# Mixing weights on four row quarters of the systolic array, in the opening of an adaLN + FFN kernel on one Trainium2 core

## What is computed

```python
# mixing by condition, the part that the change touches
h = gelu(cond_128 @ W0 + b0); h = gelu(h @ W1 + b1)
att = softmax(h @ W2 + b2)                       # 64 x 8
agg_w = einsum('bk,koi->boi', att, weight)       # 64 x 32 x 32, the mixing weights
agg_b = att @ bias_k                             # 64 x 32
y = einsum('boi,bih->boh', agg_w, x) + agg_b[:, :, None]
# gated FFN with quantised weights and low-rank parts, 512 -> 1376 -> 512
qlinear(v) = v @ ((q - 7.5) * scale * 0.005).T + 0.02 * (v @ A @ B)
x = x + qlinear_down(silu(qlinear_gate(y)) * qlinear_up(y))
# grouped convolution of 9 taps along the width, context added, then an fp8 linear layer
x = x + fp8_linear(conv(x) + ctx + bias)
```

## Time and profile before

| | us |
|---|---|
| median of three runs | 373.33 |
| the profiled execution | 373.0 |
| its span, first to last instruction | 371.2 |
| TensorE busy | 361.3 |
| VectorE busy | 243.1 |
| ScalarE busy | 190.3 |
| GpSimd busy | 78.7 |
| share of the chain that ended last, TensorE | 93% |

### The profile page before, as it was taken

One profiled execution on the slowest core, in us unless ns is written; L12 is line 12 of the kernel. 1 busy time (PEld: TensorE's weight loads), 2 busy tenths in 40 slices (PEclk: granted clock), 3 DMA queues, 4 the chain that ended last, 5 costly groups with the idle time before them and its releaser, 6 DMA issues.

```text
span 371.2 us, 5798 instructions
## 1 busy us (share of the span) xinstructions
PE 361.3 (97%) x2209; PEld 301.0 (81%) x2210; DVE 243.1 (65%) x409; ACT 190.3 (51%) x345; POOL 78.7 (21%) x68
## 2 busy tenths in 40 slices
PE   7999999999999999999999999999999999998994
PEld 3777887999888879998888789988888899997331
DVE  4949989436576664265766642737888822688995
ACT  5667797202656653035555641345667510066972
POOL 4000000021222332111422241113233221142040
PEclk9999999999999999999999999999999999999999
DMA  7997693495220000222200002326000299968288
GB/s 230 344 270 245 192 299 119 152 302 87 42 44 0 0 2 1 44 42 42 44 1 2 0 0 33 52 44 155 0 3 1 65 276 279 195 153 195 85 188 267
DMA packets 82476, 41.72 MB, mean 112 GB/s; under 512 B 52417, under 2 KB 72785, under 8 KB 82321
## 3 DMA queue, kind: packets, MB, share of 16 engines
q1 hardware_dynamic: 69072, 37.70, 37.4%
q10 hardware_dynamic: 12624, 1.82, 3.1%
q0 software_dynamic: 752, 1.84, 2.8%
HBM read 26.55 MB, written 14.80 MB: 111 GB/s over the span
## 4 chain that ended last, share of the span: by engine, by line
PE 93%; DVE 4%; ACT 1%; issue 1%; DVEq 0%
PE ps L675 44%; PE ps L660 25%; PE ps L690 6%; PE ps L608 4%; PE ps L710 3%; PE ps L870 3%; PE ps L666 2%; PE ps L712 2%; PE ps L850 1%; PE ps L623 1%; PE ps L568 1%; DVE v_plus L1506 1%; DVE q_fp L1525 1%; DVE amax L1383 0%; DVE v_plus L1513 0%
## 5 line engine op out<-in xcount | busy, mean ns | idle before, releaser
L660 PE MATMUL ps<-down_w,h_hi 128*128 128x288 f32 (+1 forms) x352 | 76.2, 297 | 0.0
L660 PE MATMUL ps<-down_w,h_lo 128*128 128x288 f32 (+1 forms) x352 | 74.7, 293 | 0.0
L675 PE MATMUL ps<-x_hi,gate_w 128*128 128x512 f32 (+1 forms) x176 | 69.9, 397 | 0.0
L675 PE MATMUL ps<-x_lo,gate_w 128*128 128x512 f32 (+1 forms) x176 | 69.6, 396 | 0.0
L675 PE MATMUL ps<-x_hi,up_w 128*128 128x512 f32 (+1 forms) x176 | 69.6, 396 | 0.0
L675 PE MATMUL ps<-x_lo,up_w 128*128 128x512 f32 (+1 forms) x176 | 69.3, 394 | 0.0
L1146 POOL TENSOR_TENSOR h_lo<-a_buf,h_hi 128x512 fp32r<-128x512 f32 (+1 forms) x33 | 42.7, 1295 | 90.0 <-ACT h_hi L984 90.0
L660 PEld LDWEIGHTS ps<-down_w,h_hi 128*128 128x128 f32 (+1 forms) x352 | 57.2, 189 | 1.1
L660 PEld LDWEIGHTS ps<-down_w,h_lo 128*128 128x128 f32 (+1 forms) x352 | 56.1, 188 | 0.0
L1435 DVE TENSOR_TENSOR a_buf<-a_buf,b_buf 128x512 f32<-128x512 f32 (+1 forms) x44 | 49.0, 1113 | 9.2 <-ACT a_buf L1050 8.1
L1157 POOL TENSOR_TENSOR x_nat<-y_buf,x_nat 128x512 f32<-128x512 f32 x15 | 20.8, 1385 | 117.0 <-DVE y_buf L1314 117.0
(11 more groups left out here) (196 smaller groups left out, 486.5 us busy)
## 6 DMA issues: line engine op xcount, KB each, us to landing
x_nat<-in_x SPq DMA_DIRECT2D x4, 1024.0 KB, 6.9
out<-x_nat SPq DMA_DIRECT2D x15, 256.0 KB, 4.5
turned<-x_nat SPq DMA_DIRECT2D x12, 256.0 KB, 3.3
x_nat<-in_down_q SPq DMA_DIRECT2D x11, 256.0 KB, 4.0
x_nat<-in_gate_q SPq DMA_DIRECT2D x10, 256.0 KB, 6.4
x_nat<-in_up_q SPq DMA_DIRECT2D x10, 256.0 KB, 6.6
edges<-zeros SPq DMA_DIRECT2D x4, 512.0 KB, 9.3
xt_own<-turned SPq DMA_DIRECT2D x6, 256.0 KB, 3.4
```

Source lines behind the costliest of these rows:

```text
L660: last = mm(ps[:, 4 + 2 * (j % 2) + m, 0:HALF + R], part[0:k, ic, j * P:(j + 1) * P], down_w[0:k, ic, m, :], start=first, stop=end)
L675: last = mm(ps[0:k, bank(ic, 2 * m), :], w[:, H * ic + c * k:H * ic + (c + 1) * k], part[:, c, :], start=c == 0 and part is x1_hi, stop=c ...
```

## The change

The mixing weights are made on four quarters of 32 rows of the array. Both factors are laid out on 128 partitions, the four stacked sums once for each quarter r; quarter r of the weights holds the output channels 4o + r, and each matrix has its 32 input channels four times side by side, once for each batch of a group. So the matmul of quarter r and block o, into bank r, gives on every band of 32 partitions the weights that this batch's block of `mix` needs, and one copy per band takes all four quarters: four copies of 32 × 128 for the first tile, two on each engine, and four of 32 × 384 for the other tiles, right behind them, straight from the banks.

With it: `cond_w_parts` is made from 128 × 256 values; the zeros in `att` go, and a column of the condition pack (`att_kept`) takes their part in a new product `att_whole`; both transposes have the same input, and ScalarE's copy waits for the first alone. GpSimd's subtraction of `lr_b` also waits for `att_bias`. The four fillers behind the bias go. The chunk of `condition(0)` that goes to bank 3 waits for the four later copies. ScalarE copies `agg_b` between its two later copies and makes the high part of `lr_a` after them. On VectorE two conversions and the low part of `lr_a` move from before the first split to behind it, the third conversion behind the second split. `mix_kept` is no longer written in the opening.

```diff
-MIX_BANK, BIAS_BANK = 5, 4
-FIRST_BANK = (6, 3, 7, MIX_BANK)
+TURN_BANKS, BIAS_BANK = (6, 5), 4
+FIRST_BANK = (6, 5, 7, 3)
...
+OC = S // OB
...
-        def mix_cells(src, q, b, g0, g1):
-            cells = src[q * S:(q + 1) * S, :].rearrange("p (o g b) -> p b g o", g=GROUPS, b=GB)[:, b, g0:g1]
-            blocks = mix[b * S:(b + 1) * S, g0:g1, b * S:(b + 1) * S].rearrange("p g (o q) -> p q g o", q=OB)[:, q]
-            return blocks, cells
+        def mix_cells(b, g0, g1):
+            cells = ps[b * S:(b + 1) * S, 0:OB, :].rearrange("p r (o g b) -> p b g o r", g=GROUPS, b=GB)[:, b, g0:g1]
+            return mix[b * S:(b + 1) * S, g0:g1, b * S:(b + 1) * S].rearrange("p g (o r) -> p g o r", r=OB), cells
...
# TensorE
-            pe.wait_ge(att_zero, 1)
-            for at, to in ((PARTS // 2, 3), (0, 2)):
-                nc.tensor.transpose(ps[0:STACKED, to, 0:B], att[:, at:at + PARTS, :].rearrange("b n k -> b (n k)"),
+            for to in TURN_BANKS:
+                nc.tensor.transpose(ps[:, to, 0:B], att[:].rearrange("b n k -> b (n k)"),
                                     ident[0:B, 0:B]).then_inc(att_tr, 1)
...
-            for o in range(S // OB):
-                last = mm(ps[:, MIX_BANK, o * B:(o + 1) * B], cond_w_parts[:, o, :], att_parts[:], start=True, stop=True)
-            last.then_inc(mix_mm, 1)
+            for o in range(OC):
+                for r in range(OB):
+                    rows = slice(r * STACKED, (r + 1) * STACKED)
+                    last = mm(ps[:, r, o * B:(o + 1) * B],
+                              cond_w_parts[rows, o].rearrange("k b i -> k (b i)"),
+                              att_parts[rows, :], start=True, stop=True)
+                    if o == OC - 1:
+                        last.then_inc(mix_mm, 1)
...
-                    if to == MIX_BANK:
-                        pe.wait_ge(mix_saved, 1)
+                    if t == 0 and to == BIAS_BANK - 1:
+                        pe.wait_ge(mix_rest, GB)
...
-            keep_clock(4)
             pe.wait_ge(mix_ready, 2)
             condition(0)
...
# ScalarE
-            act.wait_ge(att_tr, 2)
-            activation(att_hi[:], ps[0:STACKED, 3, 0:B], copy).then_inc(att_hi_ready, 1)
-            act.wait_ge(mix_mm, 1)
+            act.wait_ge(att_tr, 1)
+            activation(att_hi[:], ps[:, TURN_BANKS[0], 0:B], copy).then_inc(att_hi_ready, 1)
+            act.wait_ge(mix_mm, OB)
             act.wait_ge(mix_zero, 1)
-            for q in range(2, OB):
-                for b in range(GB):
-                    last = activation(*mix_cells(ps[:, MIX_BANK, :], q, b, 0, TG), copy)
+            for b in range(2, GB):
+                last = activation(*mix_cells(b, 0, TG), copy)
             last.then_inc(mix_ready, 1)
...
+            spread_rest(2)
+            act.wait_ge(aggb_mm, 1)
+            activation(agg_b[:, 0:TILE], ps[:, BIAS_BANK, :], copy).then_inc(aggb_ready, 1)
+            spread_rest(3)
             act.wait_ge(lr_in, 16)
             activation(lr_a_w[:, :, :, 0, :], stage_lr_a[:], copy).then_inc(lra_hi, 1)
-            act.wait_ge(aggb_mm, 1)
-            activation(agg_b[:, 0:TILE], ps[:, BIAS_BANK, :], copy).then_inc(aggb_ready, 1)
-            act.wait_ge(mix_ready, 2)
-            activation(mix_kept[:], ps[:, MIX_BANK, :], copy).then_inc(mix_saved, 1)
             split_mixed(0)
...
-                    if t == 0 and 4 <= ic < 4 + OB:
-                        spread_rest(ic - 4)
...
# GpSimd
             pool.wait_ge(lrb_hi, 1)
+            pool.wait_ge(att_ready, 2)
             nc.gpsimd.tensor_tensor(lr_b_parts[:, :, 1, :], stage_lr_b[:], plain(lr_b_parts[:, :, 0, :]),
                                     ALU.subtract).then_inc(lrb_ready, 1)
...
# VectorE
-            v.tensor_copy(cond_w_hi[:], cond_w_sb[:]).then_inc(mixw_hi, 1)
             dve.wait_ge(cond_in, 16)
+            v.tensor_scalar(cond_w_hi[:], cond_w_sb[:], w_sign, None, ALU.mult).then_inc(mixw_hi, 1)
             dve.wait_ge(mixw_hi, 1)
-            v.scalar_tensor_tensor(cond_w_parts[:].rearrange("k o p -> k (o p)"), plain(cond_w_hi[:]), w_sign,
-                                   cond_w_left[:], ALU.mult, ALU.add).then_inc(mixw_ready, 1)
+            def in_places(w):
+                return w.rearrange("k (o i) -> k o i", i=S).unsqueeze(2).to_broadcast([P, OC, GB, S])
+            v.tensor_tensor(cond_w_parts[:], in_places(plain(cond_w_hi[:])), in_places(cond_w_left[:]),
+                            ALU.add).then_inc(mixw_ready, 1)
...
-            v.tensor_scalar(att[:, PARTS // 2:, :], probs[:].unsqueeze(1).to_broadcast([B, PARTS, EXPERTS]),
+            v.tensor_scalar(att[:], probs[:].unsqueeze(1).to_broadcast([B, OB * PARTS, EXPERTS]),
                             stat[:, 2:3], None, ALU.mult).then_inc(soft, 1)
             dve.wait_ge(att_tr, 2)
+            v.tensor_scalar(att_whole[:], ps[:, TURN_BANKS[1], 0:B], att_kept, None, ALU.mult).then_inc(att_whole_ready, 1)
             dve.wait_ge(att_hi_ready, 1)
-            v.scalar_tensor_tensor(att_parts[:], plain(att_hi[:]), att_sign, ps[0:STACKED, 2, 0:B], ALU.mult,
+            dve.wait_ge(att_whole_ready, 1)
+            v.scalar_tensor_tensor(att_parts[:], plain(att_hi[:]), att_sign, att_whole[:], ALU.mult,
                                    ALU.add).then_inc(att_parts_ready, 1)
...
-            dve.wait_ge(mix_mm, 1)
+            dve.wait_ge(mix_mm, OB)
             dve.wait_ge(mix_zero, 1)
-            for q in range(2):
-                for b in range(GB):
-                    last = v.tensor_copy(*mix_cells(ps[:, MIX_BANK, :], q, b, 0, TG))
+            for b in range(2):
+                last = v.tensor_copy(*mix_cells(b, 0, TG))
             last.then_inc(mix_ready, 1)
+            for b in range(2):
+                v.tensor_copy(*mix_cells(b, TG, GROUPS)).then_inc(mix_rest, 1)
...
                     if c == 0 and t == 0:
+                        convert(0)
+                        convert(1)
+                        dve.wait_ge(lra_hi, 1)
+                        v.tensor_tensor(lr_a_w[:, :, :, 1, :], stage_lr_a[:], plain(lr_a_w[:, :, :, 0, :]),
+                                        ALU.subtract).then_inc(lra_ready, 1)
+                    if c == 1 and t == 0:
                         convert(2)
...
-            convert(0)
-            convert(1)
-            dve.wait_ge(lra_hi, 1)
-            v.tensor_tensor(lr_a_w[:, :, :, 1, :], stage_lr_a[:], plain(lr_a_w[:, :, :, 0, :]),
-                            ALU.subtract).then_inc(lra_ready, 1)
             dve.wait_ge(aggb_ready, 1)
             split_mixed(0)
```

More of the change, by code:

```diff
@@ L68 @@
 ROUND_SCALE, ROUND_MIN = 2.0 ** 20, 1.5 * 2.0 ** 14
[L70 removed]
+COND_WIDTHS = (B, P, P, EXPERTS, 1, 1, EXPERTS, 1, 1, 1)
 PARTS = 4
@@ L138, in build @@
         early = ExitStack()
-        pad_gate = sb("pad_gate", [P, 2 * HC * I - 4 * (S // OB) * P], F32, early)
-        cond_w_sb = sb("cond_w_sb", [STACKED, S // OB * P], F32, early)
-        cond_w_left = sb("cond_w_left", [STACKED, S // OB * P], F32, early)
-        cond_w_hi = sb("cond_w_hi", [STACKED, S // OB * P], F32R, early)
-        cond_w_parts = sb("cond_w_parts", [STACKED, S // OB, P], F32R, early)
+        pad_gate = sb("pad_gate", [P, 2 * HC * I - (3 + GB) * OC * S], F32, early)
+        cond_w_sb = sb("cond_w_sb", [P, OC * S], F32, early)
+        cond_w_left = sb("cond_w_left", [P, OC * S], F32, early)
+        cond_w_hi = sb("cond_w_hi", [P, OC * S], F32R, early)
+        cond_w_parts = sb("cond_w_parts", [P, OC, GB, S], F32R, early)
         cond_in_sb = sb("cond_in_sb", [P, COND_COLS], F32, early)
@@ L148, in build @@
         probs = sb("probs", [B, EXPERTS], F32, early)
-        att = sb("att", [B, PARTS + PARTS // 2, EXPERTS], F32, early)
-        att_hi = sb("att_hi", [STACKED, B], F32R, early)
-        att_parts = sb("att_parts", [STACKED, B], F32R, early)
+        att = sb("att", [B, OB * PARTS, EXPERTS], F32, early)
+        att_hi = sb("att_hi", [P, B], F32R, early)
+        att_whole = sb("att_whole", [P, B], F32, early)
+        att_parts = sb("att_parts", [P, B], F32R, early)
         att_t = sb("att_t", [EXPERTS, B], F32, early)
@@ L171, in build @@
         early.close()
-        cond_sb, w0_sb, w1_sb, w2_sb, b0_sb, b1_sb, b2_sb, w_sign, att_sign = (
+        cond_sb, w0_sb, w1_sb, w2_sb, b0_sb, b1_sb, b2_sb, w_sign, att_sign, att_kept = (
             cond_in_sb[0:rows, COND_AT[n]:COND_AT[n] + COND_WIDTHS[n]]
-            for n, rows in enumerate((P, P, P, P, P, P, B, STACKED, STACKED)))
+            for n, rows in enumerate((P, P, P, P, P, P, B, P, P, P)))
         phase2 = ExitStack()
@@ L244, in build @@
         mix_mm = sem("mix_mm")
-        mix_ready, mix_saved, mix_rest = sem("mix_ready"), sem("mix_saved"), sem("mix_rest")
-        att_hi_ready, att_parts_ready, att_zero = sem("att_hi_ready"), sem("att_parts_ready"), sem("att_zero")
+        mix_ready, mix_rest = sem("mix_ready"), sem("mix_rest")
+        att_whole_ready = sem("att_whole_ready")
```

(22 more changed lines are left out.)

16 lines of the change are left out of this document (6 added, 10 removed).

## The result

| | before | after |
|---|---|---|
| median, us | 373.33 (22 runs, 372.94 to 374.54) | 374.62 (22 runs, 373.04 to 379.37) |
| ratio, 95% interval | | 1.0038 (1.0022 to 1.0054) |
| profiled execution, us (span) | 373.0 (371.2) | 375.7 (373.9) |

The account below looks back on a forecast made before the run. TensorE, busy 97% of the span, was taken to bound the kernel, so an earlier start moves everything forward. Opening −0.93, first low part +0.13, `lr_b` stall +0.1 gave −0.7: 372.6 us against the median 373.33, range 372.0 to 374.2.

Parts of the forecast that it names:

- 8.75: Opening: start of the mixing matmuls in us, +0.05 against 8.70, bounds −0.1 and +0.4.
- the lower bound: Mixing matmuls: all quarters fully side by side, 32 as long as the 8 of before, 1.07 us.
- the 1.4 taken: Mixing matmuls: 32 at L870's load distance of 0.036 us, 31 × 0.036 + 0.27 = 1.4 us.
- 0.69 and 0.6: VectorE in the opening: `att_bias` 0.69 us like the product at 33.80, in place of 1.34; two `mix` copies 0.6.
- the 11.1 of the sum: Opening: `condition(0)` starts at 11.1 in place of 12.03, the bias's matmul ending last; gain 0.93 us.
- The first low part: After VectorE's first split: low part ends at 15.5, TensorE reaches `x1_lo` at 15.5; cost 0.13 us (0 to 0.5).
- Rivals 2 and 4: 2: mixing quarters do not overlap, 374.9, chance 0.12; 4: strided copies cost whole rows, 0.60 each, 373.1, chance 0.10.
- GpSimd's wait: Before the first low-rank matmul: later `lr_b` store moves transfers 0.2 us (bounds 0 and 1.66); stall taken 0.1.
- Rival 1: First low-rank matmul: store's whole 1.66 us reaches the loads, second lands at 27.7; +0.65, 374.0; chance 0.15.
- the full queues: DMA share 1.11 from 11.5 to 14.5 us, so the later-issued store begins about when its place comes up now.

Follow-up runs that it names:

- PSUM and no wait: Changed kernel with `att_whole` in PSUM, GpSimd's wait removed and TensorE's implied waits left out: 372.24, 0.9968; repeated 372.42, 0.9969 and 372.21, 0.9969; with all TensorE waits 373.15, 1.0000.
- SBUF and no wait: Changed kernel, `att_whole` kept in SBUF, GpSimd's wait removed and TensorE's implied waits left out: 372.70, 0.9982; with all TensorE waits 373.80, 1.0018.
- the one with 40 instructions more: Changed kernel with `att_whole` in PSUM and no GpSimd wait, plus 20 matmuls of 32 columns behind the late fillers: 373.22, 1.0001.

## Why the prediction was wrong

**The opening was right, in part by luck.** The mixing starts 1.1 us behind the transposes, and those came 0.19 later in this execution (7.92; 7.73 before); 8.75 was forecast, 9.02 came. The mixing took 1.08, the lower bound, in place of the 1.4 taken: (1.08 − 0.27)/31 = 0.026 us apart. The later start (0.27) and the shorter mixing (0.3) cancel, and that the sum comes so close is luck. VectorE's and GpSimd's time lines of after bear out the steps behind it, `att_bias` at 0.68 and two copies in 0.57 where 0.69 and 0.6 were taken:

```profile
9.12 0.68 DVE L1213 TENSOR_TENSOR att_bias<-att_t,bias_k_sb 8x512 f32<-8x512 f32 x1
10.23 0.57 DVE L1219 COPY mix<-ps 32x128 f32<-32x128 f32 x2 [0.43 <-PE ps L596]
...
9.95 1.64 POOL L1132 TENSOR_TENSOR lr_b_parts<-stage_lr_b,lr_b_parts 128x688 fp32r<-128x688 f32 x1 [6.82 <-DVE att_bias L1213]
```

`condition(0)` at 10.99 is the 11.1 of the sum, with the bias's matmul in front of it. The first low part cost nothing that can be seen (0.13 taken, though its own two sides both came to 15.5): L672 on it starts at 15.50, 0.24 behind the matmul ahead of it. Rivals 2 and 4 are out.

**The step that failed is "GpSimd's wait".** Its first half held: the store came late, the issue of the loads hardly (0.2 taken, 0.18 measured). The sum then let the loads land as long behind their issue as before, and took a stall of 0.1. They landed 12.0 us behind their issue, 2.3 more, and TensorE waited 2.15; in the other four profiles of the change with this wait and nothing put in front of it, 0.63 to 1.82. By the medians the wait costs 0.7 to 2.0 us. What it had wrong stands on SP's queue behind the store: the four slot loads. The prediction put them at 0, because TensorE waits for no slot, and left out that they share the rings with `lr_b`. They were issued 1.4 to 2.1 us later, closer to the loads of `lr_b`. From 11.5 to 14.5 us the rings carried 260 GB/s at a share of 0.88, where they had carried 366 at 1.11; the 0.3 MB that are missing (106 GB/s × 3 us) come later. All profiles divide this way: 190 to 318 GB/s in that stretch in the seven with the wait, 344 to 370 in the twelve without. The change was priced by the delay of one store, when it had opened a hole in full queues. That the hole is what slows the loads is argued from these rows; no run moved the slot loads alone, so the cause behind the late landing stays open. Rival 1 had the outcome, rows of `lr_b` that land late, and 374.0 us for it, which is what the changed kernel takes with 17 packets (373.98 and 373.99). But its route, the store's whole 1.66 us passed on to the loads, is not what happened (0.18), so that its number is met is luck. The argument against it, the full queues, held for the issue of the loads and failed for their landing, and its chance of 0.15 was too low.

**A term was missing: TensorE's code.** The 40 instructions more were costed by their time on the engine alone. They bring an 18th packet of 16 KB, which in these profiles falls on a ring while it carries the last output. When it goes, the ratio of the changed kernel falls by 0.0017 to 0.0023 (from 1.0038 to 1.0021 and 1.0015); that of the kernel with PSUM and no wait falls by 0.0032 (1.0000 to 0.9968), with SBUF and no wait by 0.0036 (1.0018 to 0.9982). That is 0.6 to 1.3 us. When it comes alone, the kernel before rises by 0.0026. The Trainium skill's page "Advanced Engine Details and Errata", section "ISA Cache", gives 16 KB as 256 instructions; the traces are near it, with 4,523 instructions of TensorE in 17 packets, 266 each, and 4,562 in 18, 253 each.

The account, in ratios: opening −0.0031 (0.9969, PSUM and no wait), the wait +0.0017 to +0.0053 (0.9986 and 1.0022 less 0.9969), the packet +0.0017 to +0.0036: +0.0003 to +0.0058, where 0.0038 was measured. That the three parts are there is shown; how the median's 1.3 us divides among them is known no better than this.

## What to carry to other kernels

An engine that is made to wait holds up not only its own store but everything queued behind that store. Where the rings are full, the price can be the bytes that then meet the next critical load, and not the delay of the first transfer; the size is shown here, this reason for it is argued. To divide a loss, take fixed points of each profile (here `condition(0)`, the one wait, VectorE's last, the end) before comparing medians. Before making one instruction into four, look at the count of code packets in the profile and at what the rings carry when the next one would come: leaving out waits that others imply bought it back for nothing here. Where two engines collide, moving an operand out of SBUF can be cheaper than making one of them wait.

## What the runs showed of the hardware that was not expected

32 float32r matmuls on four row quarters take the time of 8 on one (1.08 and 1.07 us). So do their weight loads. One lasts 0.187 us in both kernels; before, on one quarter, they start (0.96 − 0.187)/7 = 0.11 us apart, and after, on four in turn, (0.97 − 0.187)/31 = 0.025. TensorE's weight loads of before, then of after:

```profile
8.69 0.96 PEld L593 LDWEIGHTS ps<-att_parts,cond_w_parts 32*128 32x128 f32 x8 [0.42 <-DVE att_parts L1199]
```

```profile
9.02 0.97 PEld L596 LDWEIGHTS ps<-att_parts,cond_w_parts 32*128 32x128 f32 x32 [0.51 <-DVE att_parts L1204]
```

VectorE's `att_parts`, with two operands in SBUF, ended within 0.1 us of GpSimd's subtraction in both runs where the two met (it took 1.30 and 1.15 us). SBUF and no wait, VectorE and GpSimd:

```profile
8.40 1.15 DVE L1202 SCALAR_TENSOR_TENSOR att_parts<-att_hi,cond_in_sb,att_whole 128x64 fp32r<-128x64 f32 x1
...
7.84 1.64 POOL L1130 TENSOR_TENSOR lr_b_parts<-stage_lr_b,lr_b_parts 128x688 fp32r<-128x688 f32 x1 [4.71 <-ACT lr_b_parts L899]
```

PSUM and no wait:

```profile
8.48 0.28 DVE L1202 SCALAR_TENSOR_TENSOR att_parts<-att_hi,cond_in_sb,ps 128x64 fp32r<-128x64 f32 x1
...
7.91 1.64 POOL L1130 TENSOR_TENSOR lr_b_parts<-stage_lr_b,lr_b_parts 128x688 fp32r<-128x688 f32 x1 [4.77 <-ACT lr_b_parts L899]
```

The first ends at 9.55, GpSimd at 9.48; with one operand in PSUM the same product takes 0.28 in the middle of GpSimd's. The Trainium skill's page "SBUF — State Buffer", section "SBUF: two separate sides", says that a VectorE instruction with two SBUF inputs and a GpSimd instruction that reads SBUF exclude each other for the whole instruction; the traces agree.

The 18th packet of code came at 364.8 to 367.9 us in every kernel that had one, also in the one with 40 instructions more (365.9).
